# The last two steps of a four-layer residual kernel: other tiles and banks for the tail, and outputs and stores by halves

## The reference

```
h   = concat(x2, hnT, tT, sT, networks) @ W1 + b1     # "hidden", several partial products
hid = h * (1 + tanh(h / 2))                           # twice silu, the factor is in W2
y   = hid @ W2 + b2                                   # "outputs"
out = x2 + norm(y) * int_g + int_be
```

## Time and profile before

| what | us |
|---|---|
| three runs | 530.65, 532.72, 549.16 |
| median | 532.72 |
| the profiled execution: its time | 533.4 |
| the profiled execution: its span | 531.6 |
| TensorE busy, of the span | 431.7 (81%) |
| VectorE | 344.4 (65%) |
| ScalarE | 281.3 (53%) |
| GpSimd | 170.8 (32%) |
| mean granted clock of TensorE | 0.901 of full speed |

### The profile page before, as it was taken

The page is one execution under the profiler, slowest core; times in us unless marked ns, Lnnn a source line. Parts: engine busy times, 40 slices in busy tenths (PEclk is TensorE's granted clock), DMA queues, the critical chain, the costliest instruction groups (busy, mean ns, idle before and its releaser), DMA issues.

```text
span 531.6 us, 10164 instructions
## 1 busy us (share of the span) xinstructions
PE 431.7 (81%) x4158; PEld 271.0 (51%) x4158; DVE 344.4 (65%) x641; ACT 281.3 (53%) x424; POOL 170.8 (32%) x144
## 2 busy tenths in 40 slices
PE   5697646862369998999999899989999898849981
PEld 3594435342335556556565565655555565424531
DVE  1264566297218778867876887788488778464933
ACT  1100289237355579667949865795777497202010
POOL 3007889120022313233142323232341430162221
PEclk9798677695659999999999999999999999869887
DMA  7649733072574657483757547473813461320011
GB/s 250 220 117 312 220 80 81 22 181 55 122 206 125 165 153 199 112 234 97 217 127 216 151 133 195 123 200 84 238 38 126 129 173 61 91 81 27 1 41 39
DMA packets 72995, 72.29 MB, mean 136 GB/s; under 512 B 54262, under 2 KB 56244, under 8 KB 72564
## 3 DMA queue, kind: packets, MB, share of 16 engines
q1 hardware_dynamic: 68660, 55.10, 39.1%
q0 software_dynamic: 3712, 12.59, 7.1%
q10 hardware_dynamic: 576, 3.95, 1.9%
HBM read 50.25 MB, written 21.23 MB: 134 GB/s over the span
## 4 chain that ended last, share of the span: by engine, by line
PE 48%; DVE 15%; ACT 13%; DMA 8%; issue 6%; SPq 6%; POOL 2%; POOLq 0%; DVEq 0%; ACTq 0%
PE ph L803 10%; ACT bd L1155 6%; PE ph L812 6%; PE pk L782 6%; PE ph L765 5%; PE pp L765 4%; PE pp L821 3%; PE pk L803 3%; DMA cols<-in_cols 2%; ACT kc L1149 2%; SPq L332 2%; DMA last_gb<-in_last_gb 2%; DVE x2T L1623 2%; DVE tT L1618 1%; DVE stats L1589 1%
## 5 line engine op out<-in xcount | busy, mean ns | idle before, releaser
L1168 ACT ACTIVATE bd<-vc,ownrow 128x512 f32<-128x512 f32 x124 | 78.4, 714 | 0.0
L1155 ACT ACTIVATE bd<-kc,ownrow 128x512 f32<-128x512 f32 x120 | 75.8, 710 | 0.3
L487 POOL TENSOR_TENSOR demod<-demod,neghalf 128x32 f32<-128x32 f32 x8 | 44.3, 5562 | 37.7 <-DVE demod L1438 37.7
L782 PE MATMUL pk<-bd,kc 128*32 128x128 f32 x1024 | 36.0, 301 | 18.3 <-ACT bd L1155 18.2
L782 PEld LDWEIGHTS pk<-bd,kc 128*32 128x32 f32 x1024 | 30.9, 122 | 29.2 <-ACT bd L1155 22.7
L525 POOL TENSOR_TENSOR attnT<-attnT,style 128x1024 f32<-128x1024 f32 x6 | 11.4, 1902 | 81.2 <-DMA attnT<-av_dram 81.2
L812 PE MATMUL ph<-w,hid 128*128 128x256 f32 x128 | 34.1, 413 | 0.0
L782 PE MATMUL pk<-bd,et 128*32 128x128 f32 x1024 | 31.6, 276 | 2.2 <-ACT bd L1168 2.2
L765 PE MATMUL pp<-xT,kwT 128*128 128x512 f32 x64 | 30.7, 625 | 2.6 <-DVE xT L1649 2.6
L765 PE MATMUL ph<-attnT,owT 128*128 128x512 f32 x48 | 24.9, 667 | 8.1 <-POOL attnT L525 4.2
L782 PEld LDWEIGHTS pk<-bd,et 128*32 128x32 f32 x1024 | 27.5, 111 | 6.0 <-issue 5.6
(11 more groups left out here) (320 smaller groups left out, 906.2 us busy)
## 6 DMA issues: line engine op xcount, KB each, us to landing
up_gb<-up_dram SPq DMA_DIRECT2D x14, 512.0 KB, 6.6
xin<-in_x SPq DMA_DIRECT2D x8, 512.0 KB, 5.7
x_dram<-x SPq DMA_DIRECT2D x8, 512.0 KB, 2.7
k_dram<-kx SPq DMA_DIRECT2D x16, 256.0 KB
kt<-k_dram SPq DMA_DIRECT2D x8, 512.0 KB, 4.0
v_dram<-kx SPq DMA_DIRECT2D x8, 512.0 KB
vt<-v_dram SPq DMA_DIRECT2D x8, 512.0 KB, 6.4
x1r<-x_dram SPq DMA_DIRECT2D x8, 512.0 KB, 4.1
```

The source lines that it names most:

```text
L487: gp.tensor_tensor(q, q, neghalf[:, 0:4 * CB].rearrange("p (l a b) -> p l a b", l=2, a=2), ALU.pow).then_inc(gs_dem, 1)
L782: ins = mm(pk[32 * r:32 * r + 32, o:o + 128], weights(h, 4 * i + r)[:, 16 * pair:16 * pair + 32], bd[:, h, 8 * i + 2 * r + pair, :], start ...
L1155: fn(bd[:, h, :, 16 * b:16 * b + 16].rearrange("p (q z) x -> p q z x", z=2), kc[:, 16 * h:16 * h + 16, :].rearrange("p q (z x) -> p q z x" ...
L1168: fn(bd[:, h, :, 16 * b:16 * b + 16], vc[:, SH * h:SH * h + SH, :], ACT.Copy, scale=ownrow[:, 1, b:b + 1]).then_inc(s, 1)
```

## The change

- `h1_6`, a view of the tile `xT` (x's tile, last used for chunk 7's keys), takes chunk 6's gathered part in `step_d7`. The wait on `d_out` before it goes; `yn` (in `h1`) is first written in `step_e7`, behind a wait on chunk 5's store.
- The output projection of chunk 7 goes to `pk` instead of P23, and stands ahead of hidden(10). It now waits for `a_av0` and `a_av1` of chunk 7, no more for `a_hnT`. The gain for `gtm` and the transposes of `x2T` come ahead of hidden(0). The first half of chunk 6's outputs moves from `step_d7` to `step_e7`.
- ACT copies `x2k` and `gtm` before it does the tanh; VectorE makes `xn` of chunk 7 before `hid` of chunk 6.
- `tT_last` (in `attnT`) and `hid_last` (in `x1r`) are tiles for chunk 7's last step. Its outputs go to P01. The second half of chunk 6's outputs, in `ph`, stands behind chunk 7's hidden(0).
- Moments, centring, sums and `rstd` of both chunks go by halves of two tiles, 4 halves in all. SyncE stores each half (256 KB) in the place of GpSimd's two stores.
- GpSimd: the onehot comes ahead of all four gathers; both adds of the last offset come behind chunk 7's normalised `h1`.

```diff
+        h1_6 = xT[:, :, :].rearrange("p a n -> p (a n)").rearrange("p (j f) -> p j f", j=NT)
+        hid_last, tT_last = x1r, attnT
 # SyncE
+            def step_e7(p):
+                for i, buf in enumerate((h1, h1, h1_last, h1_last)):
+                    j = 2 * (i % 2)
+                    after(sp, v_yr, 2 * p + i, 2)
+                    sp.dma_start(out[:, p * NT + 2 * i:p * NT + 2 * i + 2, :], buf[:, j:j + 2, :]).then_inc(d_end, 16)
 # GpSimd, step_d7 and step_e7
+                after(gp, d_idx, d, 32)
+                after(gp, p_sg, d - 1)
+                settled(gp)
+                gp.tensor_scalar(onehot[0:24, :], idx_rows[:, :], rowclass[0:24, :], None, ALU.is_equal).then_inc(g_oh, 1)
                 after(gp, g_pw, d)
                 after(gp, v_h1, d - 1)
                 settled(gp)
                 gp.indirect_dma_start(pwgb[:, 3, :], ...)
...
-                after(gp, v_hT, e)
-                gp.tensor_tensor(xin[:, :, :], xin[:, :, :], last_gb[:, 1:2, :].to_broadcast([128, NT, D]), ALU.add
-                                 ).then_inc(g_x2b, 1)
...
-                after(gp, v_yr, p, 4)
-                gp.dma_start(out[:, p * NT:p * NT + NT, :], yn[:, :, :]).then_inc(d_out, 16)
-                after(gp, v_hT, e)
+                after(gp, v_hn, e, 4)
+                gp.tensor_tensor(xin[:, :, :], xin[:, :, :], last_gb[:, 1:2, :].to_broadcast([128, NT, D]), ALU.add
+                                 ).then_inc(g_x2b, 1)
                 gp.tensor_tensor(x2k[:, :, :], x2k[:, :, :], last_gb[:, 1:2, :].to_broadcast([128, NT, D]), ALU.add
                                  ).then_inc(g_x2b, 1)
+                for i in range(4):
+                    j = 2 * (i % 2)
+                    after(gp, v_mv[2], 2 * p + i, 2)
+                    settled(gp)
+                    gp.tensor_scalar(ve[:, 2, j:j + 2], mv[:, 2, j:j + 2, 1], LN_EPS, None, ALU.add).then_inc(g_ve[2], 1)
+                    after(gp, g_ve[2], p + i)
+                    gp.tensor_tensor(rstd[:, 2, j:j + 2], ve[:, 2, j:j + 2], neghalf[:, 0:2], ALU.pow).then_inc(g_rs[2], 1)
 # TensorE, step_d7
                 hidden(2, tT, p_ht)
+                after(pe, v_sT, e)
                 after(pe, v_hn, e, 4)
-                turn(P23, h1, p_hnT)
-                after(pe, v_sT, e)
+                turn(P23, h1_6, p_hnT)
+                after(pe, a_av0, d)
+                after(pe, a_av1, d)
+                after(pe, g_ao, d)
+                proj(pk, owT, attnT, p_o)
                 hidden(10, xnT, p_hs)
-                after(pe, g_ao, d)
-                after(pe, a_hnT, d - 1)
-                proj(P23, owT, attnT, p_o)
                 after(pe, v_hT, e)
-                hidden(0, hnT, p_hid, stop=True)
+                after(pe, g_oh, d)
+                gain(P01, D, p_tg)
+                after(pe, a_hnT, e)
                 after(pe, v_x2, d, 2)
                 ... transposes of x2T into P23
+                hidden(0, hnT, p_hid, stop=True)
                 hidden(4, x2T, p_hx, start=True, bank=pk)
-                after(pe, v_hid, e)
-                outputs(0)
                 after(pe, v_xn, d, 4)
                 after(pe, a_gtm, d)
                 turn(P01, xn, p_xnT)
 # TensorE, step_e7
                 ... onehot into pk
+                after(pe, v_hid, p)
+                outputs(0).then_inc(p_y, 1)
                 after(pe, a_xnT, e)
                 gain(P01, 0, p_cg)
                 gain(P23, 2 * D, p_sg)
-                outputs(1).then_inc(p_y, 1)
                 after(pe, v_tT, e)
-                hidden(2, tT, p_ht, bank=pk)
+                hidden(2, tT_last, p_ht, bank=pk)
...
                 hidden(0, hnT, p_hid, stop=True, bank=pk)
+                outputs(1).then_inc(p_y, 1)
                 after(pe, v_hid, e)
-                after(pe, v_yn, e - 1, 4)
-                outputs(0)
-                outputs(1).then_inc(p_y, 1)
+                outputs(0, P01, hid_last).then_inc(p_y, 1)
+                outputs(1, P01, hid_last).then_inc(p_y, 1)
 # VectorE, step_d7
-                after(ve_, d_out, e - 1, 16)
...
-                tt(by_batch2(tmp_o[:, :, :]), by_batch2(halves(P23)), per_batch2(demod[:, 1, :, :], d), ALU.mult
+                tt(by_batch2(tmp_o[:, :, :]), by_batch2(halves(pk[:, :])), per_batch2(demod[:, 1, :, :], d), ALU.mult
 # VectorE, step_e7: tT_last behind the aggregates of h1_last, then its normalisation, sT, hnT, and
+                moments(0, y)
+                after(ve_, d_out, p - 1, 16)
+                centred(0, y, yn)
+                summed(0, yn, xin)
                 after(ve_, a_th, e)
+                stt(hid_last[:, :, :], th[:, :, :], 1.0, halves(pk[:, :]), ALU.add, ALU.mult).then_inc(v_hid, 1)
+                moments(1, y)
+                centred(1, y, yn)
+                summed(1, yn, xin)
+                moments(2, y_last)
+                centred(2, y_last, h1_last)
+                moments(3, y_last)
+                summed(2, h1_last, x2k)
+                centred(3, y_last, h1_last)
+                summed(3, h1_last, x2k)
```

More of the change, by code:

```diff
@@ L1324, in step_d7 @@
                 fn(hnT[:, :, :], halves(P23), ACT.Copy).then_inc(a_hnT, 1)
-                after(act, p_hid, e)
-                after(act, v_x2, min(e + 1, NC - 1), 2)
-                fn(th[:, :, :], halves(ph[:, :]), ACT.Tanh, scale=0.5).then_inc(a_th, 1)
                 after(act, p_x2k, d)
@@ L1332, in step_d7 @@
                 fn(gtm[:, :, :], halves(P01), ACT.Copy).then_inc(a_gtm, 1)
+                after(act, p_hid, e)
+                after(act, v_x2, d, 2)
+                fn(th[:, :, :], halves(ph[:, :]), ACT.Tanh, scale=0.5).then_inc(a_th, 1)
             def step_e7(e):
@@ L1798, in step_d7 @@
                     stt(x2T[:, f, :], tmp_o[:, f, :], cols[:, 6 + f:7 + f], x1r[:, f, :], ALU.add, ALU.add).then_inc(v_x2, 1)
-                after(ve_, a_th, e)
-                after(ve_, p_y, e - 1)
-                stt(hid[:, :, :], th[:, :, :], 1.0, halves(ph[:, :]), ALU.add, ALU.mult).then_inc(v_hid, 1)
                 after(ve_, a_x2k, d)
@@ L1812, in step_d7, with moments, centred, summed @@
                        ).then_inc(v_xn, 1)
+                after(ve_, a_th, e)
+                after(ve_, p_y, e - 1)
+                stt(hid[:, :, :], th[:, :, :], 1.0, halves(ph[:, :]), ALU.add, ALU.mult).then_inc(v_hid, 1)
             def step_e7(p, e):
+                y_last = P01.rearrange("p (j f) -> p j f", j=NT)
+                def moments(i, y_):
+                    js = (2 * (i % 2), 2 * (i % 2) + 1)
+                    after(ve_, p_y, p + i)
+                    for j in js:
+                        ve_.bn_stats(stats[:, 2, j, :], y_[:, j, :]).then_inc(v_bn[2], 1)
+                    after(ve_, v_bn[2], 2 * p + i, 2)
+                    settled(ve_)
+                    for j in js:
+                        ve_.bn_aggr(mv[:, 2, j, :], stats[:, 2, j, :]).then_inc(v_mv[2], 1)
+                def centred(i, y_, dst):
+                    after(ve_, v_mv[2], 2 * p + i, 2)
+                    for j in (2 * (i % 2), 2 * (i % 2) + 1):
+                        stt(dst[:, j, :], y_[:, j, :], mv[:, 2, j, 0:1], last_gb[:, 0, :], ALU.subtract, ALU.mult
+                            ).then_inc(v_yn, 1)
+                def summed(i, dst, x2):
+                    after(ve_, v_yn, 2 * p + i, 2)
+                    after(ve_, g_rs[2], p + i)
+                    after(ve_, g_x2b, p + i // 2)
+                    for j in (2 * (i % 2), 2 * (i % 2) + 1):
+                        stt(dst[:, j, :], dst[:, j, :], rstd[:, 2, j:j + 1], x2[:, j, :], ALU.mult, ALU.add).then_inc(v_yr, 1)
                 after(ve_, d_pw[0], e, 16)
@@ L1832, in step_e7 @@
                     ve_.bn_aggr(mv[:, 1, j, :], stats[:, 1, j, :]).then_inc(v_mv[1], 1)
-                after(ve_, p_sg, e)
-                tt(xnT[:, :, :], xnT[:, :, :], halves(P23), ALU.mult).then_inc(v_sT, 1)
-                after(ve_, p_y, p)
-                for j in range(NT):
-                    ve_.bn_stats(stats[:, 2, j, :], y[:, j, :]).then_inc(v_bn[2], 1)
-                after(ve_, v_bn[2], p, NT)
-                settled(ve_)
-                for j in range(NT):
-                    ve_.bn_aggr(mv[:, 2, j, :], stats[:, 2, j, :]).then_inc(v_mv[2], 1)
+                after(ve_, a_xnT, e)
+                after(ve_, a_gtm, e)
+                tt(tT_last[:, :, :], xnT[:, :, :], gtm[:, :, :], ALU.mult).then_inc(v_tT, 1)
                 after(ve_, g_rs[1], e)
@@ L1845, in step_e7 @@
                        ).then_inc(v_hn, 1)
-                after(ve_, v_mv[2], p, 4)
-                for j in range(NT):
-                    stt(yn[:, j, :], y[:, j, :], mv[:, 2, j, 0:1], last_gb[:, 0, :], ALU.subtract, ALU.mult).then_inc(v_yn, 1)
+                after(ve_, p_sg, e)
+                tt(xnT[:, :, :], xnT[:, :, :], halves(P23), ALU.mult).then_inc(v_sT, 1)
                 after(ve_, a_hnT, e)
```

65 lines of the change are left out of this document (12 added, 53 removed).

## The result

The changed kernel is faster: 518.7 us against 532.6 for the kernel before (medians of four runs each, of which three lie at 517.0 to 520.0 and three at 530.7 to 532.7), a ratio of 0.9749 with the 95% interval 0.9719 to 0.978. A second set of runs of the same kernel, timed later, gave 0.9769 (0.9749 to 0.9789). The forecast of 522.1 us was 3.4 us too slow: the result lies just inside the whole range (518.5 to 526.7), and outside the forecast's own (520.7 to 523.8). The prediction had given 0.48 to "faster by over 2%" and 0.49 to "within 2%".

A forecast was written before the change was run, and what follows sets the result against it. TensorE's last 60 us, released late by chunk 5's store, bound it. Second turn's end + 18.1 + 9.3 + 4.2 gave 518.2 to 522.45, middle 520.3, plus 0.7: 521.0, or 522.1 us against the median; range 518.5 to 526.7.

The forecast's parts named there:

- The multiply and the norm: Step d7: h1_6 in x's tile lets VectorE's multiply start 3.57 us earlier; first turn at 467.45 or 469.35, against 472.85.
- X: Step d7: VectorE finishes its four norm instructions before GpSimd's attnT multiply; normalised at 467.4, turn at 467.45.
- Y: Step d7: GpSimd's attnT multiply gets in before the norm's last instruction; normalised at 469.3, turn at 469.35.
- TensorE's order in d7: Reordered TensorE work up to the second turn's end: 17.2 us at full clock; that end moves 5.8 to 8.3 us earlier.
- rival A: Norm ahead of GpSimd's multiply and no low clock in e7: 520.0 us, 519.1 with full clock through d7; chance 0.20.
- The add on xin: GpSimd's add moves from d7 behind e7's normalisation, where TensorE-bound work covers its 2.4 us; cost nothing.
- Step e7: From the second turn's end to hid_last's end: 18.1 us at full clock, before 19.46; low clock adds 0 or 1.7.
- the add of 0.7 us for semaphore steps: Added to the whole sum for semaphore steps joined at 0.03 us: the middle 520.3 becomes 521.0.
- The end by halves: From hid_last to the last sum, VectorE-bound: 9.3 us by halves instead of 11.59, saving 2.3.
- Rival D: At the end, halves save nothing because splitting costs in fixed parts what it overlaps: +3.7, 525.8 us; chance 0.08.
- part 4: The end from hid_last on, chunks' statistics, centring and sums by halves: 9.3 us, saved 2.3; tail 4.2, saved 1.4.
- The tail: From last sum to program end: 0.05 + 2.2 landing + 1.94 behind it, 4.2 us instead of 5.64, saved 1.4.

The follow-up runs named there:

- the run with the idle add: The changed kernel plus one idle 128x1024 VectorE add before the four instructions normalising chunk 6's h1; 536.8 us in one run.
- the run with the last chunk whole: The changed kernel with chunk 7's end undone to wholes: four-tile statistics, one rstd, centring, sum and 512 KB SyncE store; 519.5 us, ratio 0.9781.
- `tT` and `sT` early: The changed kernel with step e7's tT before h1_last's statistics and sT before the wait for rstd; 513.7 and 515.1 us, ratio 0.9685.
- the two moves of the last experiments: Against the changed kernel: step e7's tT before h1_last's statistics, 517.5 us; then also sT before h1_last's normalisation, 513.7 and 515.1 us.

## Why the prediction held, and where it was off

The path was the right one, and so was the direction, though the chances had left it open (0.48 for what came, 0.49 for "within 2%"). The terms, against the values of the first trace:

- **The multiply and the norm.** Forecast: 3.57 us saved, turn at S+8.75 (X) or S+10.65 (Y). It was X, S+8.70, by a margin of 0.1 us or less between the norm's end and the landing, which no row before could have shown. The run with the idle add shows that Y happens as soon as GpSimd's data comes in the middle of the four. The even split was caution; the landing is 0.4 us later than I took it, since SyncE issued the load at S+4.98 and not at S+4.62.
- **TensorE's order in d7.** Forecast for X: P at S+27.9 with a low clock on the turn, S+27.0 without any. The two traces gave 27.81 and 27.00. The full clock was dealt with in rival A, as a side remark; it came in one of these two traces.
- **The add on xin.** Forecast cost of the move: nothing. True for the move, but the reason for it was missed: left in its place it costs 1.65 us of TensorE's time in the new order. `x2T` was "hidden" only because this add was gone.
- **Step e7.** Forecast 18.1 us, or 19.8 with a low clock; measured 20.36 with one and 18.94 without. hidden(2) started at P+4.90 instead of 4.55; the add of 0.7 us for semaphore steps covers most of what is over.
- **The end by halves.** Forecast 9.3, measured 8.84: the pow on half the columns took 0.71 us instead of 1.04. Rival D, halves that save nothing, is refuted by the run with the last chunk whole: 1.16 us and 0.84 of tail. But the 2.3 us "saved" in part 4 were put down to the halves, and of the measured 2.76 only 1.16 are theirs. The 11.59 us of the kernel before held outputs at the low clock (3.32 us instead of 1.99), and 1.6 us came back with outputs(1) in the gap before them. Rival A says that it fills a gap; the sum has no term for it, and came out right since it counts the end from `hid_last` afresh.
- **The tail.** This is the step that failed, in its size. I wrote 0.05 + 2.2 + 1.94. The landing was right (2.1), but the 1.94 us behind it are no constant of the program. They come with GpSimd's store (1.6 and 1.7 us at the barrier with it, 0.2 without, in two pairs of kernels), and 0.5 was left of them, so 1.5 us more were saved. I had the 1.94 as a plain difference, 531.6 minus the landing, and never asked what it was.

In sum, X with a low clock was forecast at 519.9 on the trace's own scale; 458.70 + 58.78 is 517.5. The 2.4 us are 0.9 (d7's clock) and 1.6 (tail) and 0.5 (pow), less 0.6 (e7). The rest of the error is the middle over X and Y and the added 0.7. The lock in the Trainium skill's rule on the port pair (SBUF — State Buffer, "SBUF: two separate sides"), which the prediction cites, showed in all six traces where the two engines met: four with the norm and two with `x2T`. Its order, first come first served, fits the start times of the norm and not those of `x2T`. The point that it leaves open, who gets in between instructions, came out for GpSimd in the one trace that asks.

What stays open: what picks the place of the low clock. In step d7 idles of 2.0 us gave it or not, 2.3 to 4.2 gave it on the projection but not on the turn, and 7.5 to 8.0 gave it on the turn and on what follows it in all of three traces. What S depends on is open too: 458.70 before, 456.42 and 458.24 in two traces of the changed kernel and 455.33 with `tT` and `sT` early, all from programs that are the same up to there. By the formula of the Trainium skill that the prediction cites (DMA: Bandwidth & Descriptors, "Anatomy of one DMA"), which is one for GpSimd's transfers, the half store would take an estimated 2.6 us; GpSimd's landed in 2.7 and SyncE's in 2.1.

## What to carry to other kernels

A wait on a buffer that a store still reads costs more than its length where it shifts other work into a collision: here 3.6 us of waiting were worth 6.2. Before a change is credited with a saving, compare traces whose TensorE ran at the same clock in the same places: the two moves of the last experiments looked worth 2.2 us and were worth 0.85. When an order is rewritten, look for GpSimd instructions on SBUF that were harmless because VectorE was idle beside them. Ask of each stretch of a tail what it consists of, and issue the very last store from an engine other than GpSimd.

## What the runs showed of the hardware

- Behind the landing of a last store that GpSimd had issued, the program took 1.9 us to end (5.64 us from the last sum with 512 KB, 4.87 with 256 KB), behind SyncE's 0.5 (3.41 and 2.58). The landing itself took 3.4 and 2.7 us from GpSimd, 2.9 and 2.1 from SyncE.
- A `scalar_tensor_tensor` of 128x512 with two SBUF inputs took 3.54 and 3.52 us instead of 0.74 beside GpSimd's add of 128x1024, in two traces. It had started 0.6 us before the add by the profile.
- GpSimd's multiply got in between two VectorE instructions of one group: the group took 3.00 us instead of 1.38, the fourth instruction 2.03 instead of 0.41 (one trace).
- One program with one idle of TensorE can have its stretch of low clock in either of two places, and the same order had it in both in another run; it cost 1.8 us on hidden(2) (5.40 against 3.60) or 1.6 on the turn and the projection together (1.91 + 4.42 against 1.06 + 3.67).
- An idle of 2.37 us before the last outputs went with 1.2 GHz on the first half of them (3.3 to 3.7 us instead of 1.99), in all four traces that have it; with other outputs in that gap the clock was full in all ten.
